# Self attention with its last pair of heads written out, and two causal corners as single float32 matmuls

## The reference

```python
h = rmsnorm(x, ln1_w)
q = (h @ wq).reshape(b, s, H, HD)      # k and v alike; H = 16, HD = 128, s = 512
scores = jnp.einsum('bqhd,bkhd->bhqk', q, k) / np.sqrt(HD).astype(np.float32)
scores = jnp.where(causal, scores, jnp.float32(-1000000000.0))
attn = jax.nn.softmax(scores, axis=-1)
ao = jnp.einsum('bhqk,bkhd->bqhd', attn, v).reshape(b, s, H * HD) @ wo
x = x + ao
```

## Time and profile before

| | |
|---|---|
| median of 3 runs | 2296.87 us (2296.24 to 2299.54) |
| the profiled execution's own time | 2293.54 us |
| its span, first to last instruction | 2291.5 us |
| TensorE busy | 2163.1 us, 94% |
| VectorE, ScalarE, GpSimd busy | 1180.4, 690.7, 989.1 us |
| mean granted TensorE clock | 0.980 |

### The profile page before, as it was taken

One profiled execution on the slowest core, in us unless ns is written; L12 is line 12 of the kernel. 1 busy time (PEld: TensorE's weight loads), 2 busy tenths in 40 slices (PEclk: granted clock), 3 DMA queues, 4 the chain that ended last, 5 costly groups with the idle time before them and its releaser, 6 DMA issues. The chain is left out here.

```text
span 2291.5 us, 40185 instructions
## 1 busy us (share of the span) xinstructions
PE 2163.1 (94%) x12066; PEld 1883.5 (82%) x12067; DVE 1180.4 (52%) x2533; ACT 690.7 (30%) x1609; POOL 989.1 (43%) x1043
## 2 busy tenths in 40 slices
PE   6879999999999999999994999979999999999997
PEld 4668888888888898888883767779999999998996
DVE  5736646564655646465665476533433333333342
ACT  5623334343333334333333211112222222222221
POOL 1225454553545454553546024424444444444443
PEclk9989999999999999999997999989999999999998
DMA  3113343343434344343336210076676676667443
GB/s 138 56 46 119 119 160 125 133 170 109 151 119 141 119 151 151 110 169 116 141 124 245 86 65 28 37 248 156 156 228 157 156 200 183 156 174 199 90 81 55
DMA packets 143417, 307.59 MB, mean 134 GB/s; under 512 B 17104, under 2 KB 17104, under 8 KB 141072
## 3 DMA queue, kind: packets, MB, share of 16 engines
q1 hardware_dynamic: 118128, 248.33, 30.9%
q0 software_dynamic: 24960, 58.21, 13.4%
q10 hardware_dynamic: 288, 0.53, 0.1%
HBM read 180.91 MB, written 126.09 MB: 134 GB/s over the span
## 5 line engine op out<-in xcount | busy, mean ns | idle before, releaser
L544 POOL TENSOR_TENSOR chunk_hi<-chunk_raw,zero 128x512 fp32r<-128x512 f32 x160 | 166.5, 1041 | 251.6 <-DMA chunk_raw<-in_whole 251.6
L1518 DVE TENSOR_TENSOR prod<-ps,silu 128x352 f32<-128x352 f32 x111 | 58.3, 525 | 313.4 <-PE ps L62 313.4
L546 POOL TENSOR_TENSOR chunk_raw<-chunk_raw,chunk_hi 128x512 fp32r<-128x512 f32 x160 | 206.8, 1293 | 12.5
L733 DVE TENSOR_TENSOR pT_lo<-ps,pT_hi 128x512 fp32r<-128x512 f32 (+3 forms) x256 | 119.8, 489 | 167.4 <-ACT pT_hi L679 167.4
L1368 POOL DMA_INDIRECT out<-y,sidx x111 | 176.5, 1590 | 54.2 <-issue 34.5
L1375 POOL TENSOR_TENSOR carry<-ident 128x1 f32<-128x1 f32 x218 | 41.2, 189 | 326.9 <-DVE gidx L1515 261.0
L707 DVE SCALAR_TENSOR_TENSOR HS<-ps,rinv,HS 128x512 f32<-128x512 f32 x260 | 176.7, 746 | 1.2 <-PE ps L62 1.2
L673 ACT ACTIVATE prob<-ps,negmax 128x512 f32<-128x512 f32 (+3 forms) x256 | 131.7, 528 | 112.1 <-DVE negmax L696 112.1
L60 PE MATMUL ps<-wv_or_qk_hi,hT_hi 128*128 128x256 f32 x512 | 145.7, 285 | 8.3 <-POOL wv_or_qk_lo L539 8.3
L60 PE MATMUL ps<-ring,xT_0hi 128*128 x448 | 150.5, 336 | 1.7 <-DMA ring<-split_weights 1.7
L60 PE MATMUL ps<-ring,hT_hi 128*128 x333 | 141.0, 423 | 7.9 <-issue 5.6
(11 more groups left out here) (293 smaller groups left out, 6216.4 us busy)
## 6 DMA issues: line engine op xcount, KB each, us to landing
ring<-split_weights SPq DMA_DIRECT2D x240, 272.0 KB, 6.8
chunk_raw<-in_whole SPq DMA_DIRECT2D x162, 256.0 KB, 2.7
split_weights<-chunk_hi SPq DMA_DIRECT2D x160, 256.0 KB, 2.4
split_weights<-chunk_raw SPq DMA_DIRECT2D x160, 256.0 KB, 2.6
xg<-in_wqk SPq DMA_DIRECT2D x17, 512.0 KB, 3.4
xg<-in_wv SPq DMA_DIRECT2D x9, 512.0 KB, 3.5
x<-in_x SPq DMA_DIRECT2D x4, 1024.0 KB, 5.6
x_spill<-x SPq DMA_DIRECT2D x4, 1024.0 KB, 3.9
```

Source lines behind the costliest of these rows:

```text
L544: nc.gpsimd.tensor_tensor(chunk_hi[k][:], chunk_raw[k][:], zero[:].to_broadcast([P, CH]), ALU.add).then_inc(chunk_high, 1)
L546: nc.gpsimd.tensor_tensor(chunk_raw[k][:].bitcast(F32R), chunk_raw[k][:], chunk_hi[k][:].bitcast(F32), ALU.subtract).then_inc(chunk_low, 1)
L733: nc.vector.tensor_tensor(pT[1][:, 0:i + 1, w], ps_t[k % 2][:, 0:(i + 1) * P].rearrange("p (j t) -> p j t", t=P), pT[0][:, 0:i + 1, w].bit ...
```

## The change

The last pair of heads leaves the loop on every engine: the body becomes a function `pair(g, last)`, called in `Fori(0, HP - 1)` and once more with `last=True`. There the projections after the last step, the third and fourth weight jobs, and the chunks beyond the 153 that exist are left out; its 13 chunks all stand behind the second job.

Two corners become one float32 matmul of 128 columns each: tile 0's scores (operands copied unsplit into `corner`), and the last key tile of the product with V (operands `v_last` and `p_last`, copied unsplit). `qkT`, `v` and `pT` keep only what the split products still need. ScalarE therefore does extra copies: `corner` ahead of each `qkT_hi`, `v_last` ahead of every second `v_hi`, `p_last` ahead of a step's first `pT_hi`; the split copies beside them, and VectorE's low parts of them, get narrower (except `qkT` of the keys, m = 1).

```diff
+def high_qk(nc, qkT, corner, m, bank):
+    w, scale = slice(P if m == 0 else 0, S), SCALE if m == 0 else 1.0
+    nc.scalar.mul(corner[:, m, :], bank[:, 0:P], scale)
+    return nc.scalar.mul(qkT[0][:, m, w], bank[:, w], scale)
+
+def low_qk(nc, qkT, m, bank):
+    w = slice(P if m == 0 else 0, S)
+    return nc.vector.scalar_tensor_tensor(out=qkT[1][:, m, w], in0=bank[:, w], scalar=SCALE if m == 0 else 1.0,
+                                          in1=qkT[0][:, m, w].bitcast(F32), op0=ALU.mult, op1=ALU.subtract)
...
-        width = [max(2, i + 1) * P for i in range(ST)]
-        first = [0, P, 2 * P, 2 * P]
+        width = [(i + 1) * P for i in range(ST)]
+        first = [0, P, 2 * P, 3 * P]
...
+        LAST_JOBS, LAST_CHUNKS = 2, -(-NE * EW // CH) - HP_CHUNKS * (HP - 1)
...
-            with sp.Fori(0, HP) as g:
-                for job in range(JOBS):
+            def pair(g, last=False):
+                for job in range(LAST_JOBS if last else JOBS):
...
-                    for c in CHUNKS_AFTER_LOAD[job]:
+                    for c in () if last else CHUNKS_AFTER_LOAD[job]:
                         store_chunk(g, c)
+                for c in range(LAST_CHUNKS) if last else ():
+                    store_chunk(g, c, c + 2 < LAST_CHUNKS)
+
+            with sp.Fori(0, HP - 1) as g:
+                pair(g)
+            pair(HP - 1, last=True)
...
+                        if i == 0:
+                            nc.tensor.matmul(ps_s[0][:, 0:P], corner[:, 0, :], corner[:, 1, :], start=True, stop=True).then_inc(pe_s, 1)
+                            continue
...
-                    for c in range(DC):
+                    for c in range(DC) if more else ():
                         project(*nxt, 0, c)
...
+                        if j == ST - 1:
+                            ended = nc.tensor.matmul(o, v_last[:, b, hh * HD:(hh + 1) * HD], p_last[:], start=False, stop=True)
+                            continue
...
+                    if v % 2:
+                        nc.scalar.copy(v_last[:, v // 2, :], ps_p[1][:, 2 * HD:4 * HD])
+                    nc.scalar.copy(v_s[0][:, v_split(v), :], ps_p[v % 2][:, v_width(v)].rearrange("p (k n) -> p k n", n=2 * HD)).then_inc(act_v, 1)
...
+                        split = min(i + 1, ST - 1)
+                        if i == ST - 1:
+                            nc.scalar.copy(p_last[:], ps_t[k % 2][:, i * P:S])
+                        nc.scalar.copy(pT[0][:, 0:split, i * P:(i + 1) * P],
+                                       ps_t[k % 2][:, 0:split * P].rearrange("p (j t) -> p j t", t=P)).then_inc(act_t, 1)
```

More of the change, by code:

```diff
@@ L361, in _ @@
                 act.wait_ge(pe_nq, m + 1)
-                nc.scalar.mul(qkT[0][:, m, :], ps_qk[m][:], SCALE if m == 0 else 1.0).then_inc(act_nq, 1)
+                high_qk(nc, qkT, corner, m, ps_qk[m]).then_inc(act_nq, 1)
             normed_x1(NB - 1)
@@ L560, in _, with pair @@
             nc.gpsimd.memset(rinv[:], 0.0).then_inc(pool_0, 1)
-            with pool.Fori(0, HP) as g:
-                for job in range(JOBS):
+            def pair(g, last=False):
+                for job in range(LAST_JOBS if last else JOBS):
                     pool.wait_ge(ld_raw[job % 2], 32 * g + 16 * (job // 2) + 32)
@@ L572, in _ @@
                     split(job % 2, [flat_qk[1], flat_o, flat_qk[0], flat_v][job], EARLY + JOBS * g + job)
-                    for c in CHUNKS_AFTER_JOB[job]:
+                    for c in () if last else CHUNKS_AFTER_JOB[job]:
                         split_chunk(g, c)
+                for c in range(LAST_CHUNKS) if last else ():
+                    split_chunk(g, c)
+            with pool.Fori(0, HP - 1) as g:
+                pair(g)
+            pair(HP - 1, last=True)
         @block.tensor
@@ L591, in _, with pair @@
             pe.wait_ge(pool_0, 1)
-            with pe.Fori(0, HP) as g:
+            def pair(g, last=False):
                 pe.wait_ge(pool_lo, ONE + JOBS * g + EARLY)
@@ L608, in _ @@
                     nxt = ((s + 1) % STEPS // NB, (s + 1) % NB)
+                    more = s + 1 < STEPS or not last
                     pe.wait_ge(dve_qk, ONE + 2 * n + 2)
@@ L634, in _ @@
                         for j in range(i + 1):
-                            last = nc.tensor.transpose(ps_t[k % 2][:, j * P:(j + 1) * P], prob[i][:, j * P:(j + 1) * P], ident[:])
-                        last.then_inc(pe_t, 1)
-                        for c in [(), (0, 1), (2,), (3,)][k]:
+                            ended = nc.tensor.transpose(ps_t[k % 2][:, j * P:(j + 1) * P], prob[i][:, j * P:(j + 1) * P], ident[:])
+                        ended.then_inc(pe_t, 1)
+                        for c in [(), (0, 1), (2,), (3,)][k] if more else ():
                             project(*nxt, 1, c)
@@ L648, in _ @@
                             pe.wait_ge(dve_t, ONE + ST * n + ST)
-                        last = nc.tensor.matmul(o, v_hi, p_lo, start=False, stop=j == ST - 1)
-                    last.then_inc(pe_o, 1)
+                        nc.tensor.matmul(o, v_hi, p_lo, start=False, stop=False)
+                    ended.then_inc(pe_o, 1)
+            with pe.Fori(0, HP - 1) as g:
+                pair(g)
+            pair(HP - 1, last=True)
             pe.wait_ge(dve_o, ONE + STEPS * HP)
@@ L710, in _, with pair @@
             dve.wait_ge(pool_0, 1)
-            with dve.Fori(0, HP) as g:
+            def pair(g, last=False):
                 for v in range(VG):
                     dve.wait_ge(act_v, ONE + VG * g + v + 1)
-                    nc.vector.tensor_tensor(v_s[1][:, 2 * v:2 * v + 2, :], ps_p[v % 2][:].rearrange("p (k n) -> p k n", k=2),
-                                            v_s[0][:, 2 * v:2 * v + 2, :].bitcast(F32), ALU.subtract).then_inc(dve_v, 1)
+                    nc.vector.tensor_tensor(v_s[1][:, v_split(v), :], ps_p[v % 2][:, v_width(v)].rearrange("p (k n) -> p k n", n=2 * HD),
+                                            v_s[0][:, v_split(v), :].bitcast(F32), ALU.subtract).then_inc(dve_v, 1)
                 for s in range(STEPS):
                     n = STEPS * g + s
+                    more = s + 1 < STEPS or not last
                     if s == 0:
@@ L732, in _ @@
                         w = slice(i * P, (i + 1) * P)
-                        nc.vector.tensor_tensor(pT[1][:, 0:i + 1, w], ps_t[k % 2][:, 0:(i + 1) * P].rearrange("p (j t) -> p j t", t=P),
-                                                pT[0][:, 0:i + 1, w].bitcast(F32), ALU.subtract).then_inc(dve_t, 1)
-                        if k == 1:
-                            low_qk(0, 2 * n + 3)
-                    low_qk(1, 2 * n + 4)
+                        split = min(i + 1, ST - 1)
+                        nc.vector.tensor_tensor(pT[1][:, 0:split, w], ps_t[k % 2][:, 0:split * P].rearrange("p (j t) -> p j t", t=P),
+                                                pT[0][:, 0:split, w].bitcast(F32), ALU.subtract).then_inc(dve_t, 1)
+                        if k == 1 and more:
+                            of_qk(0, 2 * n + 3)
+                    if more:
+                        of_qk(1, 2 * n + 4)
                     dve.wait_ge(act_o, ONE + n + 1)
                     nc.vector.tensor_tensor(oT[1][:], ps_o[:], oT[0][:].bitcast(F32), ALU.subtract).then_inc(dve_o, 1)
+            with dve.Fori(0, HP - 1) as g:
+                pair(g)
+            pair(HP - 1, last=True)
             add_output(0, STEPS * HP)
```

72 lines of the change are left out of this document (38 added, 34 removed).

## The result

The changed kernel takes 2273.71 us (median of 4 runs, 2270.03 to 2275.30); before, in the same comparison, 2296.55 us (4 runs). The ratio is 0.9897, 95% interval 0.9885 to 0.9909: 22.8 us faster by the medians, between 21 and 26 by the interval. The forecast was a gain of 25.9 us and a median of 2271.0 us. The profiled execution took 2274.86 us, its span is 2273.0 us.

A forecast was written before the change was run, and what follows sets the result against it. TensorE, busy 94% of the span, was taken as the bound, with an exponential chain in 56 of 64 steps and a chunk tail. Terms 13.3 + 2.25 + 7.7 + 2.7 - 0.1 = 25.9 us gave 2271.0 us, range 2266 to 2280.

The forecast's parts named there:

- (a): End of self attention: with fewer chunks in the last pair, VectorE instead of chunk loading ends the stage; gain 13.3 us.
- (b): Last self-attention step: without its 24 projection matmuls the product with V starts earlier, bound by a chain; gain 2.25 us.
- (c): Product with V, every step: one float32 matmul replaces three, saving 0.12 us, extra copies cancelled by narrower pT_lo; gain 7.7 us.
- (d): Scores in 8 first steps of pairs: float32 corner saves 0.12 us and v_lo comes earlier, 0.22; gain 2.7 us.
- (e): Pair's second copy in each engine's program costs nothing, stall at most 0.3 us; two extra copies ending cross attention cost 0.1.
- A: Rival on both float32 corners: they bring nothing, through matmul price or late ScalarE copies; 2279.8 us, chance 0.14.
- B: Rival on the float32 corners: four separate passes cost 0.44 us each, lengthening steps by 0.1; 2286.2 us, chance 0.08.
- D: Rival on the float32 corners: every record exposed, 0.92 us a corner, kernel slower at 2320.6 us, chance 0.02.
- C: Rival on the stage after self attention: its earlier start changes the clock, router matmuls slower; 2273.6 to 2276 us, chance 0.14.
- E: Rival on the end of self attention: last pair's chunks still end last, so the tail stays; 2284 us, chance 0.02.

The follow-up runs named there:

- chunks_only: Changed kernel without both float32 corners and with the last step's projections and copies kept, so only chunks and two weight jobs are cut; 2282.81 us, ratio 0.9941.
- last_pair: Changed kernel without both float32 corners: last pair written out and cut, last step's projections removed; 2285.69 us, ratio 0.9962 to the kernel before.
- keep_matmuls: Changed kernel, but TensorE still makes the 24 projection matmuls after the last step, which nobody reads; 2274.55 us, ratio 0.9899 to the kernel before.
- fillers: Changed kernel plus 12 unread matmuls of 512 columns in the last step where TensorE would wait; two runs, 2273.23 and 2270.25 us.
- score_corner: Kernel before plus only the scores' float32 corner, all pairs in the loop, 160 chunks; 2296.72 us, ratio 1.0004.
- av_corner: Kernel before plus only the float32 corner of the product with V, all pairs in the loop, 160 chunks; 2283.94 us, ratio 0.9945.
- before_again: The unchanged kernel before, run once more for a second profile; self attention 1071.20 us, router stage 47.71 us.

## Why the prediction came out as it did

The time lay in the range, 2.7 us above the forecast; the terms did less well than their sum.

- **(a) the chunks, 13.3.** Held. From the last `oT_hi` to the next stage 18.9 and 18.5 us before, 5.47 in `chunks_only`: 13.2 on average; by the medians `chunks_only` is 12.8 us faster. In its profile VectorE's last instruction is followed by the next stage within 0.3 us. The six chunks that stood behind the fourth weight job were six of the seven that hold no weights (20 chunks for each of 8 pairs, 153 with weights), so the tail was padding alone.
- **(b) the last step's projections, 2.25.** This step failed. The timing chain was right: the product with V starts at 1186.42, 2.9 us after the fourth update of `HS` (forecast: 2.7), and with the clock held up the step is 1.80 us shorter. What was missing is the clock. The matmuls were not only work but what TensorE did between two waits; without them the product with V ran at half clock (3.7 us from its start to the cast instead of 2.1), and in three of four profiles what follows it too. In the changed kernel's first profile the step gains 0.37 and the stretch from `oT_hi` to the next stage, 5.47 us in `chunks_only`, takes 7.37, so (b) is -1.5; in the second 0.70 is gained and nothing lost behind it, so +0.7. Instead of the 2.25 that the forecast put there, -0.4 on average over the two, with -1.6 in `last_pair`. By the medians it is -2.9 between `last_pair` and `chunks_only`, and nothing that can be told between the changed kernel (2273.71, 2274.16) and `keep_matmuls` (2274.55); so the sign of the loss is shown for `last_pair`, and its size varies from run to run. The Trainium skill says in "TensorE: Matmul & The Clock Gate", section "What's actually happening", that the throttled state is the default and activity releases it. These runs agree: a granted clock of 0.50 in this stretch without the matmuls, 1.00 with them or with fillers.
- **(c) the corner of the product with V, 7.7.** Right mechanism, sized too small: 0.12 a step forecast, 0.13 to 0.16 measured, so 64 x 0.14 = 9.0. I had subtracted starts in TensorE's stream, where the corner costs 0.28 and not the 0.23 that I took, so that way of counting gives only 0.07. The chain to the exponentials hangs on the product's end, and there the corner gives 0.13. The cancelling of the copies and of the narrower `pT_lo` held, with a slack of 0.05 that I had put at none.
- **(d) the scores' corner and v_lo, 2.7.** Held: the stretch over a pair's start went from 36.70 to 36.24, 0.32 more than a step's 0.14, so 8 x 0.32 = 2.6. `score_corner` shows 0.10 of it for the corner, `av_corner` 0.20 for the earlier `v_lo`.
- **(e) the second copy of the pair, nothing.** In doubt: the stages behind the router are some 2.4 us longer in the kernels with the last pair written out. The forecast had bounded a stall at the entry of the copy by 0.3, and this time stands elsewhere. That writing the pair out is its cause is likely from the thirteen profiles, not shown.
- Sum of (a) to (d) as measured: 13.2 - 0.4 + 9.0 + 2.6 = 24.4, against 24.1 in the traces of the two stages. The medians' 22.8 is less, as the longer rest of the kernel would have it. So the forecast came near in part by luck: (c) 1.3 above its term made up for half of the 2.7 that (b) fell short.
- **Rivals.** A and B are out: the corners pay, steps are 0.14 shorter and not 0.1 longer. D fell with them. C named the clock, but as something that the next stage would suffer from an earlier start; that stage takes as long as before on average, and it was the hole in the last step that brought the low clock, inside self attention in both profiles. E did not occur.

## What to carry to other kernels

Before removing work from a busy engine, see whether it stands between two waits: if the waits stay, what follows may run at the lower clock, and its price (here, against the kernel with fillers, 3.3 us in one profile and 1.1 in another, against a gain of 1.8) belongs into the sum. Price an edit on a dependent chain by the distance from it to its consumer, not by TensorE's start-to-start distance. And cut first what ends last: 13 of 23 us came from chunks of padding behind a late job of GpSimd, which is busy for 43% of the span.

## Not expected of the hardware

- The two records of a float32 matmul of 128 columns take 0.28 us in TensorE's own stream, counting the wider gap that they leave ahead of the matmuls behind them, and deliver their result after 0.42.
- The clock fell to its lower level (granted clock 0.50) at the end of self attention, a stage in which it is 1.00 from 160 us to 1180, behind a stretch in which TensorE was busy for 1.78 and then 2.04 of 3.0 us, in the end with transposes alone; 12 matmuls that nobody reads kept it at 1.00 in both runs.
- One execution differs from another of the same program by 2 us from where the clock comes up in the first stage (before and `before_again`), and by 1.5 to 1.9 us in the router stage, again with the clock: 0.50 or 1.00 from 9 to 13 us behind its start.
